# A PSUM copy moved to the head of VectorE's loop body, and an input load moved ahead of a transpose in SyncE's queue

## The reference

```
xn    = layernorm(x)                                   # mean 0, variance 1
B, C  = xn @ W2 + b2, xn @ W3 + b3                     # 16 values each
delta = softplus(xn @ W1 + b1)                         # 1024 values
s     = sum_n C[n] * xn * delta * B[n]                 # = xn * delta * dot(B, C)
xq    = fake_quant_4bit(xn @ H)                        # H: Hadamard 1024x1024, one scale per row
g     = silu(xq @ ternary(weight).T)
out   = x + s * g
```

## Time and profile before

| what | value |
|---|---|
| median of 12 runs | 512.72 us (511.33 to 514.6) |
| the profiled execution | 508.92 us |
| its span on the slowest core (core 3), first to last instruction | 507.4 us |
| spans of the 8 cores | 505.7 to 507.4 us |
| mean granted TensorE clock, die 0 and die 1 | 0.884 and 0.881 |
| HBM read and written per core | 25.93 MB and 16.78 MB, 84 GB/s over the span |

### The profile page before, as it was taken

How to read it: one execution, slowest core, us unless ns; L and a number is a source line. 1 busy time by engine, 2 the same in 40 slices (tenths; PEclk the granted TensorE clock), 3 DMA queues, 4 the chain that set the end, 5 groups by cost and what they waited for, 6 DMA issues and landing times.

```text
span 507.4 us, 7129 instructions; the slowest of 8 cores (505.7 to 507.4 us)
## 1 busy us (share of the span) xinstructions
PE 345.8 (68%) x1696; PEld 148.1 (29%) x1696; DVE 347.1 (68%) x632; ACT 344.0 (68%) x393; POOL 257.3 (51%) x183
## 2 busy tenths in 40 slices
PE   0004260699888877798897989889797978884400
PEld 0001130344333333333342434333343333431100
DVE  0508888264787788878878787887878886576260
ACT  0622232568978897888878888887888787776220
POOL 6000152011456665666666666665666566774653
PEclk9998566599898999989989989989898999996655
DMA  7993322152445565557664756555656534324111
GB/s 131 251 224 90 94 90 45 31 95 62 96 113 131 133 137 123 129 122 141 153 146 104 143 139 138 131 132 124 126 124 126 125 83 85 84 74 113 41 52 72
DMA packets 80972, 57.77 MB, mean 114 GB/s; under 512 B 70435, under 2 KB 70564, under 8 KB 80932
## 3 DMA queue, kind: packets, MB, share of 16 engines
q1 hardware_dynamic: 72916, 34.19, 36.0%
q0 software_dynamic: 8016, 23.14, 14.0%
HBM read 25.93 MB, written 16.78 MB: 84 GB/s over the span
## 4 chain that ended last, share of the span: by engine, by line
DVE 33%; PE 22%; ACT 18%; issue 9%; DMA 8%; POOL 6%; DVEq 1%; SPq 1%; ACTq 0%; POOLq 0%
DVE o3s L33 5%; ACT esb L33 4%; PE psO L285 4%; PE psO L286 4%; DVE t3b L33 3%; PE psZ L264 3%; PE psZ L265 3%; DVE prod L33 3%; DVE tbf L33 3%; DVE t1b L33 3%; POOL ob L33 3%; DMA xb<-x 3%; PE psXH L308 3%; DMA xnT<-xnb 3%; POOL t4b L33 3%
## 5 line engine op out<-in xcount | busy, mean ns | idle before, releaser
L33 POOL TENSOR_TENSOR t4b<-t3b,o3s 128x1024 f32<-128x1024 f32 x32 | 75.2, 2349 | 122.8 <-DVE t3b L33 122.8
L285 PE MATMUL psO<-ternT,xqT 128*128 128x512 bf16 x256 | 100.3, 392 | 13.0 <-DMA xqT<-xqb 9.4
L264 PE MATMUL psZ<-W1c,xnT 128*128 128x512 bf16 x256 | 100.1, 391 | 0.5 <-DVE bcw L33 0.5
L286 PE MATMUL psO<-ternT,xqT 128*128 128x512 bf16 x256 | 99.9, 390 | 0.0
L265 PE MATMUL psZ<-W1c,xnT 128*128 128x512 bf16 x256 | 99.4, 388 | 0.0
L308 PE MATMUL psXH<-Hs,uT 128*128 128x512 bf16 x128 | 57.1, 446 | 39.6 <-ACT xqm L33 37.5
L33 POOL TENSOR_TENSOR ob<-xb,t4b 128x1024 f32<-128x1024 f32 x32 | 76.1, 2379 | 4.6
L33 ACT ACTIVATE esb<-psO,nsa 128x1024 f32<-128x1024 f32 x32 | 35.6, 1114 | 39.1 <-DVE o3s L33 38.9
L310 PE MATMUL psXH<-Hs,vT 128*128 128x512 bf16 x128 | 57.1, 446 | 0.0
L33 POOL TENSOR_TENSOR uT<-xnT 128x512 bf16<-128x512 bf16 x32 | 37.2, 1161 | 36.5 <-DMA xnT<-xnb 35.6
L33 ACT ACTIVATE esb<-psZ 128x1024 f32<-128x1024 f32 x32 | 32.7, 1023 | 28.8 <-PE psZ L267 26.4
(11 more groups left out here) (53 smaller groups left out, 507.1 us busy)
## 6 DMA issues: line engine op xcount, KB each, us to landing
xb<-x SPq DMA_DIRECT2D x32, 512.0 KB, 5.1
out<-ob POOLq DMA_DIRECT2D x32, 512.0 KB, 6.2
wfst<-wf POOLq DMA_DIRECT2D x8, 512.0 KB, 4.1
W1c<-w POOLq DMA_DIRECT2D x8, 256.0 KB, 18.3
Hs<-hpk SPq DMA_DIRECT2D x1, 512.0 KB
xnT<-xnb SPq DMA_TRANSPOSE x32, 3.1
xqT<-xqb SPq DMA_TRANSPOSE x32, 4.1
W23s<-w POOLq DMA_DIRECT2D x1, 64.0 KB, 3.4
```

Of the source, the lines that this page charges most:

```text
L33: inst = fn(*a, **kw)
L264: pe.matmul(psZ1[:, 0:512], lh, W1c[ic][:, 0:512], start=(ic == 0), stop=False)
L285: pe.matmul(ps[:, 0:512], lh, ternT[:, ic * DM:ic * DM + 512], start=(ic == 0), stop=(ic == KC - 1))
L286: last = pe.matmul(ps[:, 512:1024], lh, ternT[:, ic * DM + 512:(ic + 1) * DM], start=(ic == 0), stop=(ic == KC - 1))
```

## The change

Two blocks are moved as they are; no instruction, buffer or semaphore is added or dropped.

- On SP, the load of tile c+5, with its wait on `sVOUT` (tile c-6), stands ahead of the transpose `xnT` of tile c+2 instead of behind it.
- On DVE, the copy `o3s` of tile c-3, with its waits on `sPEO3` and `sVOUT` (tile c-5), stands at the head of the step, ahead of `mx`, instead of just ahead of `t1b`.

```diff
@@ sync
             for c in range(-4, nt + 4):
+                t = c + 5
+                if 5 <= t < nt:
+                    if t >= 11:
+                        sp.wait_ge(sVOUT, t - 10)
+                    sp.dma_start(out=xbuf[t % 11][:], in_=x_hbm[t * 128:(t + 1) * 128, :]).then_inc(sLDa[t % 11], 16)
                 t = c + 2
                 if 0 <= t < nt:
                     sp.wait_ge(sXNB, t + 1)
...
                                  transpose=True).then_inc(sTXNa[t % 3], 16)
-                t = c + 5
-                if 5 <= t < nt:
-                    if t >= 11:
-                        sp.wait_ge(sVOUT, t - 10)
-                    sp.dma_start(out=xbuf[t % 11][:], in_=x_hbm[t * 128:(t + 1) * 128, :]).then_inc(sLDa[t % 11], 16)
                 t = c - 1
@@ vector
+                w_ = c - 3
+                if 0 <= w_ < nt:
+                    dv.wait_ge(sPEO3, w_ + 1)
+                    if w_ >= 2:
+                        dv.wait_ge(sVOUT, w_ - 1)
+                    dv.tensor_copy(o3s[w_ % 2][:], psO3x[w_ % 2][:], _inc=(sO3S, w_ + 1))
                 u = c - 1
                 if 0 <= u < nt:
                     dv.wait_ge(sPEXH, u + 1)
...
-                w_ = c - 3
-                if 0 <= w_ < nt:
-                    dv.wait_ge(sPEO3, w_ + 1)
-                    if w_ >= 2:
-                        dv.wait_ge(sVOUT, w_ - 1)
-                    dv.tensor_copy(o3s[w_ % 2][:], psO3x[w_ % 2][:], _inc=(sO3S, w_ + 1))
                 w2 = c - 4
```

## The result

| | before | after |
|---|---|---|
| median of the runs | 512.70 us | 592.64 us (592.13 to 596.44, 11 runs) |
| profiled execution, span on its slowest core | 508.92, 507.4 us | 593.19, 591.7 us |
| mean granted TensorE clock, die 0 and die 1 | 0.884, 0.881 | 0.818, 0.821 |

The changed kernel is slower by a ratio of 1.157, with a 95% interval of 1.155 to 1.159. The forecast was 593 us, range 585 to 612.

The account below looks back on a forecast made before the run. DVE was taken to set the pace at 11.96 us a step. The turn became 15.46 us: 23 turns to 491.0, drain 72.0, end 24.7, span 587.7, execution 589.2, scaled to the median 593 us; range 585 to 612.

Parts of the forecast that it names:

- The loop: `t3b`, `t4b`, `ob`, `o3s` and DVE's step close on themselves; one turn is one tile, 15.46 us against 11.96.
- The give-back of 1.9 us: DVE's step: of the 5.39 us wait, 1.9 come back, nearly all because POOL no longer disturbs DVE.
- the margin of 0.2 us between `vT` and `cc`: POOL's `vT` ends 3.5 us into DVE's new step, `cc` comes at about 3.7: cost 0, at most 0.3 a step.
- First copy that waits: Step 5: `o3s` of tile 2, where the new wait first occurs, put at 135.4 us.
- The drain: Steps 28 to 33, as the pipeline empties: together 72.0 us, the last `o3s` starting at 563.0.
- the multiplier: Total: 589.2 us scaled by 512.72 / 508.92, since the profiled execution was faster than the median, giving 593 us.
- the terms of the range: Start 2 either way, step 4 1.5 either way, turns -3 to +11, ratio to the median 2 either way: 585 to 612.
- SP: The load's earlier issue on SP: 0, since nothing waits for it; in the start bounded at 2 us either way.
- PE at the lower clock: PE idles some 6 us each turn; if all its matmuls run slow, 17.5 us a tile, about 650 us; chance 0.05.
- Not slower: The wait on DVE costs little, if `sVOUT` comes within 1.9 us of `t3b`: about 485 us; chance 0.03.
- partly hidden: DVE's waits for PE in the full pipeline swallow the new wait; turn about 13 us, 524 us; chance 0.04.
- The second rival: The wait on DVE costs little; with ACT's 10.75 us as next bound, up to 28 us saved, about 485; chance 0.03.

Follow-up runs that it names:

- the third buffer: The changed kernel with a third `o3s` buffer, so that the copy waits for `ob` of tile c-6 instead of c-5: 511.75 us, ratio 0.994.
- `t4b` twice: The changed kernel with POOL's `t4b` done twice in a row: 672.80 us, ratio 1.313.
- the load alone: The kernel before with only the SP half of the change, the copy `o3s` where it was: 515.18 us, ratio 1.001.
- the one-input forms: The kernel before with `cc`, `msq`, `var`, `nmrs`, `prod` reading one tensor from SBUF, the second operand a per-partition scalar or from PSUM: 502.43 us, ratio 0.980.

## Why the prediction was right

**The loop and its terms.** The step on which all rests, that `t3b`, `t4b`, `ob`, `o3s` and DVE's step close on themselves, is shown by the third buffer (open the loop, the loss goes) and by `t4b` twice (lengthen it, the whole length shows). Its terms, from the turn shown above:

| term | forecast | after |
|---|---|---|
| `o3s` and `t1b` | 2.67 | 1.34 + 1.34 = 2.68 |
| `t3b` | 1.28 | 1.28 |
| end of `t3b` to `o3s` | 5.39 | 5.39 |
| `mx` to `xsm` | 2.64 | 2.64 |
| `xsm` to `bcw` | 2.64 | 2.64 |
| `bcw` to `t1b` | 0.84 | 0.85 |
| turn | 15.46 | 15.48 |

The wait was taken from the drain of before, where the same order already stood; it held to a hundredth, and to 0.02 in the mean of all 30 waits (5.41). The give-back of 1.9 us was right as well: `msq` is at 0.16 and `prod` at 0.17 in the turn, and the margin of 0.2 us between `vT` and `cc` held.

**The total.** First copy that waits: 136.15 against 135.4. The 23 turns from it to the `o3s` at 494.68, those of steps 5 to 27, average 15.59 and not 15.46, 3.0 us more. (The 15.49 given above, between `t3b` starts, includes step 28, which lacks some 2.4 us.) The drain took 72.3 against 72.0 and the end 24.7 as before. That makes a span of 591.7 where I had 587.7. Most of the missing 3 us comes from turns such as 291.86 to 307.55, 15.69 us, where DVE stood 0.30 us before `sa` with its own `mxc` as the only releaser; such gaps are in the trace of before too, and I left them out of the sum.

```profile
294.99 0.15 DVE L33 TENSOR_SCALAR sa<-mxc 128x1 f32<-128x1 f32 x1 [0.30 <-DVE mxc L33]
```

Such gaps go with the place in DVE's list and not with the tile's work: in the traces of before, of after and of the third buffer alike there is one ahead of the 186th of DVE's 632 instructions, which is a `bcw` before and a `nmrs` in the other two, and in the trace of after they mostly recur every 51 or 52 instructions, while a turn has 18. Their cause stays open.

**A cancelling error.** I multiplied by 512.72 / 508.92 because the profiled execution of before was faster than its median. After, the profiled one took 593.19 and the median is 592.64. So the multiplier, worth 4.4 us, had no counterpart, and it hid the 4 us that the sum was short. The hit to within a microsecond is in that part luck. Two sums were also written down wrong: 589.2 x 512.72 / 508.92 is 593.6, and the terms of the range reach up to about 610, not 612. The result lies well inside either.

**SP.** Priced at 0 with 2 us either way: the load alone measured 1.001, interval 0.999 to 1.002, about plus or minus 1 us.

**The rivals.** *PE at the lower clock:* half of its condition came true. PE is idle 4.68 us in this turn, and the burst after it begins at the lower level of the clock, 1.2 GHz (granted clock 0.50 from 297.5 to 301.3): pairs of matmuls 0.85 us apart, then, from 301.65 on, at the upper level, 2.4 GHz (1.00 from 301.9 to 304.5), 0.43 apart:

```profile
297.54 0.59 PE L308 MATMUL psXH<-Hs,uT 128*128 128x512 bf16 x1 [4.68 <-ACT xqm L33]
...
299.20 0.63 PE L308 MATMUL psXH<-Hs,uT 128*128 128x512 bf16 x1
300.05 0.63 PE L308 MATMUL psXH<-Hs,uT 128*128 128x512 bf16 x1
...
301.65 0.38 PE L264 MATMUL psZ<-W1c,xnT 128*128 128x512 bf16 x1
302.08 0.38 PE L264 MATMUL psZ<-W1c,xnT 128*128 128x512 bf16 x1
```

The mean granted clock from 139 to 494 us is 0.83. `bcw` waited for PE in only 6 steps, 12.7 us of it a single wait: the slow burst is hidden by the longer turn. The Trainium skill, as cited in the prediction ("TensorE: Matmul & The Clock Gate", section "What's actually happening"), has the clock throttled until activity releases it; the trace agrees with it, a burst that starts slow and then recovers. *Not slower, partly hidden:* each of the 30 waits is there in full; neither happened. The second rival's price was also too high: it took ACT's busy time, 10.75 us a tile, as the next bound, but where ACT was the bound its turn was 11.49 us, because busy time leaves out the gaps between instructions (0.10 us between `xqb` and `esb` in the rows above).

## What to carry to other kernels

Before an instruction is moved up on an in-order engine, ask of each of its waits which instruction of the same engine that wait depends on through other engines; if it is the one just executed, the round trip can show in full, as it did here, and the drain or the start of the same kernel may have its price in one row. To have the earlier place without the wait, give the tile one more buffer: the same position then cost nothing in the total, and with the stalls beside POOL removed it was the fastest kernel here. A gain on one engine is worth what the next bound leaves: by the mean durations of their groups the one-input forms took some 1.2 us a step off DVE (0.55 of it at `prod`, 0.46 at `msq`), and 0.3 us a step came through (12.27 to 11.99, means over the eight cores) until the copy stood ahead of `bcw`. Such small differences need all cores: the slowest ones of the two traces alone show 0.1 (12.21 to 12.13), and in the kernel before the mean turn of a core lies anywhere from 12.20 to 12.37.

## What the runs showed of the hardware

A second operand that is given as a per-partition scalar from SBUF didn't stall beside POOL: `cc`, `msq`, `var` and `nmrs` in that form were between 212 and 218 ns in all 32 tiles, 24 of the `cc` and 25 of the `msq` wholly inside one of POOL's tensor instructions, while as two-tensor instructions they ranged up to 2.28 us (`cc`) and 1.53 us (`nmrs`) in the kernel before. The form costs some 50 ns more than an undisturbed two-tensor instruction (214 against 160 ns). And such a stall ends with POOL's instruction, however small DVE's own work is: a one-column `cc` took 1.44 us and ended within 0.01 us of `ob`, and in the kernel before each of the 75 instructions of these five kinds (`cc`, `msq`, `var`, `nmrs`, `prod`) that took over 0.25 us ended within 0.05 us of the end of one of POOL's tensor instructions.
